# Two-layer graph attention, layer 0: the four small transfers of a tile are begun by GpSimd in its own queue, SyncE begins only the adjacency chunks

## Chip, cores and metric

The kernel runs on one core of one Trainium2 chip. The metric is the device time of one launch in microseconds (us).

## The reference

Two layers of graph attention over N = 8192 nodes of 128 features. The adjacency has about one edge in a thousand (eight per row).

```python
def _L0_gnn_ref(h, adj, Ws, Wt, Wc):
    Whs = h @ Ws
    Wht = h @ Wt
    e = jnp.einsum('nh,mh->nm', Whs, Wht)
    z = jnp.where(adj > 0, e, NEG)
    alpha = jax.nn.softmax(z, axis=-1)
    return alpha @ (h @ Wc)

def _L1_gnn_ref(h, adj, W, a):
    Wh = h @ W
    e = jax.nn.leaky_relu((Wh @ a[:128, 0])[:, None] + (Wh @ a[128:, 0])[None, :], negative_slope=0.2)
    attention = jax.nn.softmax(jnp.where(adj > 0, e, NEG_INF), axis=1)
    return jax.nn.elu(attention @ Wh)

h = jnp.maximum(_layernorm(x, axis=-1), 0.0)
x = x + _L0_gnn_ref(h, adj, L0_gnn_Ws, L0_gnn_Wt, L0_gnn_Wc)
h = jnp.maximum(_layernorm(x, axis=-1), 0.0)
x = x + _L1_gnn_ref(h, adj, L1_gnn_W, L1_gnn_a)
```

## The kernel before

**Stages.** The program first loads all rows of x, normalizes them and projects them (up to about 100 us). Then comes the stage that this change touches: layer 0 over 64 tiles of 128 query rows each (about 100 to 1088 us). After it the rows of layer 1 are prepared, and layer 1 runs over the same 64 tiles. Layer 1 doesn't read the adjacency again: layer 0 has stored, for every tile, which key blocks were picked (`sel_pick`) and the mask of the picked keys (`sel`).

**What a tile of layer 0 does.** A tile's adjacency, 128 queries by 8192 keys as int32, is 4 MB. It comes in four chunks of 1 MB (`load_chunk`, L394 to L398), into four buffers (`adj_st`). VectorE converts each chunk to 8 bits (`convert`, L1284). It reduces the tile to an indicator (L1290, one such instruction in a tile, so its start is a good mark for the tile's period), and makes a matrix `pick` from a prefix sum (L1307). TensorE uses `pick` to gather the keys (L650), values (L662) and mask (L677) that have an edge. ScalarE takes these from PSUM: keys L970, values L975, mask L982 (`take_mask`, two halves in a tile, into one of two buffers of `m_sel`). TensorE computes the scores (L694 to L699; their L696 reads the mask), VectorE reads them with their maximum (L1318), ScalarE takes the exponential (L990), TensorE turns the weights (L708, taken by L997) and weighs the values (L720), and VectorE writes the tile's result `y_t` (`finish`, L1361).

**Software pipeline.** Every engine runs `tile_sweep(engine, step)`: steps i = 0 to 66, where step i works on tile i in its front part, on tile i-1 in its middle part, on tile i-2 in its rear part and on tile i-3 in its ending. Steps 0 to 3 and 62 to 66 are written out, those between run in a hardware loop of two steps. The order within a step is written by hand and differs by engine. On VectorE it is: convert chunk 0 of tile i+1; indicate tile i; finish tile i-3; convert chunk 1; four tiny operations of tile i-2 and one that adds x (`without_edges`, L1352); place; read two scores of tile i-1; pick of tile i; convert chunks 2 and 3; read the other two scores.

**The four small transfers of a tile**, all begun by SyncE (SP) between the chunks:

- `store_y` (L406): `y_t` to `x_mid`, 64 KB, after `y_ready` (the finish of tile i-3);
- `load_x` (L401): x of tile i-1 to `x_t`, 64 KB, no wait;
- `store_pick` (L417): `pick` of tile i-1 to `sel_pick`, 256 KB, after `pick_ready`;
- `store_mask` (L411): `m_sel` of tile i-2 to `sel`, 256 KB, after `m_evac` (both halves of L982).

SP's order in a step:

```python
if later:
    load_chunk(i + 2, 0)
if ending(i):
    store_y(i - 3, 1 - b)
if later:
    load_chunk(i + 2, 1)
if within(i, 3, TILES + 1):
    load_x(i - 1, 1 - b)
if middle(i):
    store_pick(i - 1, 1 - b)
if rear(i):
    store_mask(i - 2, b)
if later:
    load_chunk(i + 2, 2)
    load_chunk(i + 2, 3)
```

A chunk load waits until VectorE has converted what was in its buffer. In the other direction ScalarE's `take_mask` waits for `m_out`: before it writes the first half of a tile's mask, the store of the mask two tiles before must have landed, since there are two buffers. Each of the other three has two buffers as well: `pick_out` is waited for by L1307, `y_out` by L1361, `x_in` by L1352. GpSimd (POOL) makes a few constants at the start (its last is L548) and then only waits for the end of the layer.

Of the kernel before, what the change touches and what calls it, by code (L numbers as in the profile page):

```python
# [16 lines left out]
P = 128  # L17
# [9 lines left out]
SLOPE = 0.2  # L27
EPS = 1e-5
# [12 lines left out]
def gnn_kernel(nc, x, adj, adjB, Ws, Wt, Wc, W1, a1, out, x_mid, sel, sel_pick):  # L41
    N = x.shape[0]
    TILES = N // P
# [10 lines left out]
    with ExitStack() as ctx:  # L54
# [253 lines left out]
        def within(t, lo, hi):  # L308

            return not isinstance(t, int) or lo <= t < hi  # L310
# [14 lines left out]
        def middle(i):  # L325
            return within(i, 1, TILES + 1)
# [4 lines left out]
        def ending(i):  # L331
            return within(i, 3, TILES + 3)
# [44 lines left out]
        def _(sp):  # L377
# [22 lines left out]
            def load_x(t, b):  # L400
                sp.dma_start(x_t[:, b, :], x[bass.ts(t, P), :]).then_inc(x_in[b], 16)  # L401

            def store_y(t, b):

                sp.wait_ge(y_ready, t + 1)
                sp.dma_start(x_mid[bass.ts(t, P), :], y_t[:, b, :]).then_inc(y_out[b], 16)  # L406

            def store_mask(t, b):

                sp.wait_ge(m_evac, t * 2 + 2)  # L410
                sp.dma_start(sel[bass.ds(t, 1), :, :].rearrange("o p n -> p (o n)"),  # L411
                             m_sel[:, b, :, :].rearrange("p s w -> p (s w)")).then_inc(m_out[b], 16)

            def store_pick(t, b):

                sp.wait_ge(pick_ready, t + 1)
                sp.dma_start(sel_pick[bass.ds(t, 1), :, :].rearrange("o p n -> p (o n)"), pick_w[:, b, :]  # L417
                             ).then_inc(pick_out[b], 16)

            def tile_io(i, b):  # L420
                later = within(i, 0, TILES - 2)
                if later:
                    load_chunk(i + 2, 0)
                if ending(i):
                    store_y(i - 3, 1 - b)
                if later:
                    load_chunk(i + 2, 1)
                if within(i, 3, TILES + 1):
                    load_x(i - 1, 1 - b)
                if middle(i):  # L430
                    store_pick(i - 1, 1 - b)
                if rear(i):
                    store_mask(i - 2, b)
                if later:
                    load_chunk(i + 2, 2)
                    load_chunk(i + 2, 3)
# [10 lines left out]
            load_x(0, 0)  # L447
            load_x(1, 1)
# [88 lines left out]
        def _(pool):  # L537
# [11 lines left out]

            def mask(tau, m):  # L550
# [17 lines left out]

            by_choice(pool, lambda: None, all_keys)
# [1117 lines left out]
```

## Time and profile before

| | us |
|---|---|
| three runs: median (lowest to highest) | 1651.59 (1649.45 to 1652.6) |
| the profiled execution, its own time | 1654.9 |
| its span, from first to last instruction | 1653.2 |
| busy: TensorE / VectorE / ScalarE / GpSimd | 1415.0 / 1447.7 / 893.3 / 1.5 |
| mean granted TensorE clock, as a share of full speed | 0.957 |
| bytes moved | 363.11 MB, mean 220 GB/s |

The profiled execution took 3.3 us more than the median, and 1.7 us more than its span. All transfers run on 16 DMA engines. All those that the program begins are in one queue, q1, which is SP's. Times in the sections that follow count from the span's start. "To landing" is the time from the start of the instruction that begins a transfer until its semaphore is complete.

### The profile page before, as it was taken

What the parts mean: (1) busy time and instruction counts of PE and PEld (TensorE: products, weight loads), DVE (VectorE), ACT (ScalarE), POOL (GpSimd) and SP (SyncE); (2) the same over time, 40 slices, a digit from 0 to 9 for tenths busy, and PEclk for the clock granted to TensorE, in tenths of its full rate; (3) what the DMA queues carried; (4) which work ended last, traced back from release to release, by engine and by line L of the source; (5) the groups of instructions that cost most, each with busy time, mean ns of one, the idle gap of its engine ahead of it and who ended that gap; (6) DMA issues with size and microseconds to landing.
All of it is one profiled execution on the core that took longest, in us unless ns stands there. A gap on an engine that the chain in (4) does not pass through costs nothing.

```text
span 1653.2 us, 78949 instructions
## 1 busy us (share of the span) xinstructions
PE 1415.0 (86%) x31882; PEld 1212.3 (73%) x32010; DVE 1447.7 (88%) x3171; ACT 893.3 (54%) x1872; POOL 1.5 (0%) x11
## 2 busy tenths in 40 slices
PE   2848899999999999899999999966888879889886
PEld 1536777777877788777877777744888878778776
DVE  5777799999999999999999999635999999999997
ACT  2725566666666666666666666666433333333332
POOL 0000000000000000000000000000000000000000
PEclk9968999999999999999999999979999989989988
DMA  6067799999999999999999999420332322332331
GB/s 211 0 259 252 281 326 320 326 330 324 319 340 329 327 328 314 331 325 330 328 326 332 330 327 322 139 57 6 106 95 84 98 91 81 92 92 80 97 91 44
DMA packets 114297, 363.11 MB, mean 220 GB/s; under 512 B 11504, under 2 KB 44528, under 8 KB 81392
## 3 DMA queue, kind: packets, MB, share of 16 engines
q1 hardware_dynamic: 114160, 361.02, 64.2%
q8 instruction: 118, 1.93, 0.5%
q14 instruction: 19, 0.16, 0.0%
HBM read 319.03 MB, written 41.94 MB: 218 GB/s over the span
## 4 chain that ended last, share of the span: by engine, by line
PE 34%; DVE 29%; issue 17%; DMA 12%; ACT 4%; DVEq 2%; SPq 2%; ACTq 0%
DMA sel<-arena 10%; PE ps L802 8%; DVE arena L1455 8%; PE ps L720 7%; DVE arena L1290 5%; DVE arena L1284 4%; PE ps L708 4%; PE ps L791 3%; DVE arena L1318 3%; PE ps L699 2%; PE ps L650 2%; DVE arena L1463 2%; PE ps L662 2%; PE ps L696 2%; ACT arena L990 2%
## 5 line engine op out<-in xcount | busy, mean ns | idle before, releaser
L1284 DVE TENSOR_SCALAR arena<-arena 128x2048 fp8e4<-128x2048 int32 x256 | 306.5, 1219 | 26.2 <-PE ps L677 14.0
L802 PE MATMUL ps<-arena 128*128 128x129 f32 x2048 | 266.1, 292 | 38.6 <-DVE arena L1463 38.5
L802 PEld LDWEIGHTS ps<-arena 128*128 128x128 f32 x2048 | 254.2, 205 | 48.8 <-DVE arena L1463 44.6
L1455 DVE TENSOR_SCALAR arena<-arena 128x128 f32 (+1 forms) x1024 | 268.4, 339 | 20.4 <-ACT arena L1039 20.4
L720 PE MATMUL ps<-arena 128*128 128x128 f32 x2048 | 271.6, 281 | 0.8 <-issue 0.8
L720 PEld LDWEIGHTS ps<-arena 128*128 128x128 f32 x2048 | 248.3, 192 | 4.3 <-issue 1.0
L970 ACT ACTIVATE arena<-ps 128x512 f16<-128x512 f32 x256 | 152.6, 596 | 180.0 <-PE ps L650 180.0
L997 ACT ACTIVATE arena<-ps 128x512 f32<-128x512 f32 x256 | 153.5, 600 | 130.3 <-PE ps L708 130.2
L1318 DVE CUSTOM_DVE_ANT_0 arena<-ps,arena 128x512 f32<-128x512 f32 x256 | 168.6, 686 | 19.5 <-PE ps L699 16.5
L791 PE MATMUL ps<-arena 128*32 128x131 f16 x8192 | 156.6, 228 | 32.6 <-issue 21.6
L1039 ACT ACTIVATE arena<-ps 128x393 f32<-128x393 f32 (+1 forms) x384 | 149.2, 462 | 49.6 <-PE ps L791 49.3
L791 PEld LDWEIGHTS ps<-arena 128*32 128x32 fp8e4 x8192 | 133.2, 99 | 52.3 <-issue 37.1
L662 PE MATMUL ps<-arena 128*32 128x128 f16 x8192 | 164.4, 222 | 6.3 <-issue 6.3
L708 PE MATMUL ps<-ident,arena 128*128 128x128 f32 x1024 | 162.9, 282 | 7.0 <-ACT arena L990 2.6
L650 PEld LDWEIGHTS ps<-arena 128*128 128x128 f16 x4096 | 130.8, 96 | 51.4 <-issue 9.0
L1047 ACT ACTIVATE arena<-ps 128x129 f32<-128x129 f32 x64 | 17.9, 279 | 271.1 <-PE ps L802 266.2
L699 PE MATMUL ps<-arena 128*128 128x512 f16 x512 | 155.8, 387 | 3.9 <-issue 3.9
L975 ACT ACTIVATE arena<-ps 128x512 f32<-128x512 f32 x256 | 152.3, 595 | 0.4 <-PE ps L662 0.4
L1463 DVE SCALAR_TENSOR_TENSOR arena<-arena 128x1024 f32<-128x1024 fp8e4 x128 | 150.5, 1216 | 0.0
L650 PE MATMUL ps<-arena 128*128 128x32 fp8e4 x4096 | 144.6, 177 | 6.7 <-DVE arena L1307 3.8
L990 ACT ACTIVATE arena<-arena,neg_max 128x1024 f32<-128x1024 f32 x128 | 146.0, 1141 | 4.4 <-DVE neg_max L1328 4.4
L1307 DVE TENSOR_TENSOR arena<-arena 128x2048 fp8e4<-128x2048 f16 x64 | 146.3, 2286 | 0.1
(139 smaller groups left out, 1537.4 us busy)
## 6 DMA issues: line engine op xcount, KB each, us to landing
arena<-in_adjB SPq DMA_DIRECT2D x256, 1024.0 KB, 7.6
sel_pick<-arena SPq DMA_DIRECT2D x64, 256.0 KB, 8.0
sel<-arena SPq DMA_DIRECT2D x64, 256.0 KB, 8.0
arena<-sel_pick SPq DMA_DIRECT2D x64, 256.0 KB, 3.1
arena<-sel SPq DMA_DIRECT2D x64, 256.0 KB, 2.7
x_t<-in_x SPq DMA_DIRECT2D x64, 64.0 KB, 7.9
x_mid<-y_t SPq DMA_DIRECT2D x64, 64.0 KB, 4.8
arena<-x_mid SPq DMA_DIRECT2D x8, 512.0 KB, 4.4
```

Of the source, the lines that this page charges most:

```text
L650: last = nc.tensor.matmul(kg_ps[:, k * SLOT:(k + 1) * SLOT], kp[:, g * SB + k, :], pick[:, b, g * SB + k, :], start=True, stop=True)
L662: last = nc.tensor.matmul(vg_ps[g % 2][j * SLOT:(j + 1) * SLOT, s * D:(s + 1) * D], pick[:, b, k, :], c_vals[:, k, l * D:(l + 1) * D], sta ...
L699: last = nc.tensor.matmul(dst, rows[:, bass.ts(t, P)], k_sel[:, q * GW:(q + 1) * GW], start=False, stop=(n == 1), skip_group_check=True)
L708: last = nc.tensor.transpose(pt_ps[:, k * P:(k + 1) * P], zc[:, (4 * g + k) * P:(4 * g + k + 1) * P], ident[:, :])
L720: last = nc.tensor.matmul(pv_ps, p_T[:, g % 2, k * P:(k + 1) * P], v_sel[:, b, s, :], start=(s == 0), stop=(s == SB - 1), skip_group_check ...
L791: last = nc.tensor.matmul(xg_ps[g % 3][j * SLOT:(j + 1) * SLOT, at:at + XW], pick[:, b, s * QB + j, :], wv[:, s * QB + j, l, :], start=(l ...
L802: last = nc.tensor.matmul(xv_ps[b], w_msk[:, b, s, :], x1_sel[:, b, s, 0:VW], start=(s == 0), stop=(s == SB - 1))
L990: nc.scalar.activation(half, half, ACT.Exp, bias=neg_max[:, 0:1], scale=1.0 / SCORE, accum_out=sums[:, 0, h:h + 1]).then_inc(p_done, 1)
L1284: nc.vector.tensor_scalar(mask_8[:, b, c * QCH:(c + 1) * QCH, :], adj_st[:, c, :, :], 0.0, 1.0, ALU.is_gt, ALU.add, saturate=False).then_i ...
L1318: nc.vector.tensor_tensor_reduce(out=zc[:, q * GW:(q + 1) * GW], in0=s_ps[q % 2], in1=zero_b, scale=1.0, scalar=LOWEST, op0=ALU.subtract, ...
L1455: last = nc.vector.tensor_scalar(w_raw[:, s, :], own, x1_sel[:, b, s, D + 2:D + 3], x1_sel[:, b, s, D + 1:D + 2], ALU.mult, ALU.max)
L1463: nc.vector.scalar_tensor_tensor(w_msk[:, b, at, :], m_in8[:, b, at, :], -1.0, w_raw[:, at, :], ALU.add, ALU.mult).then_inc(w_ready, 1)
```

## The change

SP's step keeps the four chunks alone. The four helpers move to GpSimd's program, in the same order among themselves, with the same waits, and GpSimd runs them in the same `tile_sweep`. Ahead of each transfer stands an increment of a semaphore that nobody in this stage waits for (`pool_settled`). The first two loads of x are begun by GpSimd after its constants, where SP began them behind the chunks of tile 0. Two constants (`SHIFT`, `TINY`) are added and not used.

```diff
             def tile_io(i, b):
-                later = within(i, 0, TILES - 2)
-                if later:
-                    load_chunk(i + 2, 0)
-                if ending(i):
-                    store_y(i - 3, 1 - b)
-                if later:
-                    load_chunk(i + 2, 1)
-                if within(i, 3, TILES + 1):
-                    load_x(i - 1, 1 - b)
-                if middle(i):
-                    store_pick(i - 1, 1 - b)
-                if rear(i):
-                    store_mask(i - 2, b)
-                if later:
-                    load_chunk(i + 2, 2)
-                    load_chunk(i + 2, 3)
+                if within(i, 0, TILES - 2):
+                    for c in range(4):
+                        load_chunk(i + 2, c)
...
             for c in range(4):
                 load_chunk(0, c)
-            load_x(0, 0)
-            load_x(1, 1)
             sp.wait_ge(mean_ready, 1)
...
             nc.gpsimd.memset(bounds[:, :], 0.0).then_inc(const_pool, 1)
 
+            def load_x(t, b):
+                pool.sem_inc(pool_settled, 1)
+                pool.dma_start(x_t[:, b, :], x[bass.ts(t, P), :]).then_inc(x_in[b], 16)
+
+            def store_y(t, b):
+
+                pool.wait_ge(y_ready, t + 1)
+                pool.sem_inc(pool_settled, 1)
+                pool.dma_start(x_mid[bass.ts(t, P), :], y_t[:, b, :]).then_inc(y_out[b], 16)
+
+            def store_mask(t, b):
+
+                pool.wait_ge(m_evac, t * 2 + 2)
+                pool.sem_inc(pool_settled, 1)
+                pool.dma_start(sel[bass.ds(t, 1), :, :].rearrange("o p n -> p (o n)"),
+                             m_sel[:, b, :, :].rearrange("p s w -> p (s w)")).then_inc(m_out[b], 16)
+
+            def store_pick(t, b):
+
+                pool.wait_ge(pick_ready, t + 1)
+                pool.sem_inc(pool_settled, 1)
+                pool.dma_start(sel_pick[bass.ds(t, 1), :, :].rearrange("o p n -> p (o n)"), pick_w[:, b, :]
+                             ).then_inc(pick_out[b], 16)
+
+            def tile_io(i, b):
+                if ending(i):
+                    store_y(i - 3, 1 - b)
+                if within(i, 3, TILES + 1):
+                    load_x(i - 1, 1 - b)
+                if middle(i):
+                    store_pick(i - 1, 1 - b)
+                if rear(i):
+                    store_mask(i - 2, b)
...
+            load_x(0, 0)
+            load_x(1, 1)
+            tile_sweep(pool, tile_io)
             by_choice(pool, lambda: None, all_keys)
```

How it moves instructions. SP before, one step of the hardware loop from the y store to the mask's store (`in_adjB` are the chunks, `arena` the large buffer in SBUF that holds most tiles; an ISA or REGISTER_ALU row is a wait or the working out of an address). Ahead of these rows stands chunk 0, behind them chunks 2 and 3:

```order
L406 ISA [waits y_ready]
L406 DMA x_mid<-y_t 128x128
L306 REGISTER_ALU
L398 ISA [waits conv_done]
L398 DMA arena<-in_adjB 128x2048
L401 ISA
L401 DMA x_t<-in_x 128x128
L417 ISA [waits pick_ready]
L417 DMA sel_pick<-arena 128x1024
L410 ISA
L411 ISA [waits m_evac]
L411 DMA sel<-arena 128x1024
```

The change, SP, the first two chunks of the same step (line numbers are those of the changed kernel). The other two read alike:

```order
L400 ISA [waits conv_done]
L400 DMA arena<-in_adjB 128x2048
L308 REGISTER_ALU
L400 ISA [waits conv_done]
L400 DMA arena<-in_adjB 128x2048
```

SP keeps only loads that wait for VectorE's conversions; nothing on it waits for `y_ready`, `pick_ready` or `m_evac` any more. The change, POOL, the same step (before, POOL had nothing in this stage):

```order
L525 ISA [waits y_ready]
L525 DMA x_mid<-y_t 128x128
L519 ISA
L519 DMA x_t<-in_x 128x128
L538 ISA [waits pick_ready]
L538 DMA sel_pick<-arena 128x1024
L529 ISA
L531 ISA [waits m_evac]
L531 DMA sel<-arena 128x1024
```

The four transfers stand in one row on POOL, and the mask's is the last of them; all four stand behind the wait for `y_ready`.

## Rows read from the trace of the kernel before

**Rows 1.** Page part 2: rates over the span in 40 slices of 41.3 us.

```profile
PE   2848899999999999899999999966888879889886
DVE  5777799999999999999999999635999999999997
POOL 0000000000000000000000000000000000000000
DMA  6067799999999999999999999420332322332331
GB/s 211 0 259 252 281 326 320 326 330 324 319 340 329 327 328 314 331 325 330 328 326 332 330 327 322 139 57 6 106 95 84 98 91 81 92 92 80 97 91 44
```

**Rows 2.** Windows: length, busy by engine (PE, PEld, DVE, ACT, POOL), clock, DMA share, GB/s.

```profile
102.45:203.25 100.80, 76.67 (x1771) 62.86 (x1783) 77.09 (x131) 48.17 (x88) 0.00 (x0) 0.83 0.80 295
203.25:1034.13 830.88, 779.22 (x18536) 654.38 (x18644) 772.54 (x1458) 543.03 (x1008) 0.00 (x0) 1.00 0.94 327
```

**Rows 3.** Source L1290, 203 to 1035 us: min/median/max ns, first and last start.

```profile
L1290 DVE TENSOR_REDUCE arena<-arena x57: 2276/2278/2280, 203.2 to 1034.1; 128x64 f32<-128x2048 f32 x57
```

**Rows 4.** Waits, 203.25 to 1034.13 us: us in total, times, longest.

```profile
ACT arena L982 <- DMA sel<-arena: 53.8, 47, 2.2
PE ps L696 <- ACT arena L982: 39.7, 38, 1.9
...
DVE arena L1284 <- PE ps L677: 12.8, 28, 0.7
```

**Rows 5.** Timeline of VectorE, four tiles: start us, us, what.

```profile
589.03 2.28 DVE L1290 TENSOR_REDUCE arena<-arena 128x64 f32<-128x2048 f32 x1
...
603.52 2.28 DVE L1290 TENSOR_REDUCE arena<-arena 128x64 f32<-128x2048 f32 x1
...
618.23 2.28 DVE L1290 TENSOR_REDUCE arena<-arena 128x64 f32<-128x2048 f32 x1
...
620.93 0.35 DVE L1361 SCALAR_TENSOR_TENSOR y_t<-ps,inv,u_t 128x128 f32<-128x128 f32 x1 [0.19 <-issue]
...
621.64 1.21 DVE L1284 TENSOR_SCALAR arena<-arena 128x2048 fp8e4<-128x2048 int32 x1
...
627.45 2.36 DVE L1284 TENSOR_SCALAR arena<-arena 128x2048 fp8e4<-128x2048 int32 x2
...
632.73 2.28 DVE L1290 TENSOR_REDUCE arena<-arena 128x64 f32<-128x2048 f32 x1
```

**Rows 6.** Timeline of SP, one step.

```profile
621.47 0.36 SPq L406 DMA_DIRECT2D x_mid<-y_t  x1
623.01 0.33 SPq L398 DMA_DIRECT2D arena<-in_adjB  x1
623.56 0.33 SPq L401 DMA_DIRECT2D x_t<-in_x  x1
624.08 0.36 SPq L417 DMA_DIRECT2D sel_pick<-arena  x1
624.73 0.43 SPq L411 DMA_DIRECT2D sel<-arena  x1
```

**Rows 7.** Chain of waits in order of time: start us, us, what.

```profile
624.73 8.62 DMA sel<-arena
...
648.52 2.29 DVE arena L1290
...
651.22 0.36 DVE y_t L1361
```

**Rows 8.** Timeline of ScalarE: idle before it and its releaser in brackets.

```profile
633.38 0.60 ACT L982 ACTIVATE arena<-ps 128x512 f16<-128x512 f32 x1 [2.14 <-DMA sel<-arena]
```

**Rows 9.** Tile sel, 203 to 1034 us: issue ns min/median/max, then landing times.

```profile
L411 SPq DMA_DIRECT2D sel<-arena x56: 355/356/1390, 209.8 to 1025.0; - x56
...
DMA to landing us min/median/max: 5.6/8.1/8.8
```

**Rows 10.** Page part 6, transfers: count, KB each, median us to landing.

```profile
arena<-in_adjB SPq DMA_DIRECT2D x256, 1024.0 KB, 7.6
...
arena<-sel SPq DMA_DIRECT2D x64, 256.0 KB, 2.7
x_t<-in_x SPq DMA_DIRECT2D x64, 64.0 KB, 7.9
x_mid<-y_t SPq DMA_DIRECT2D x64, 64.0 KB, 4.8
```

**Rows 11.** Lines, 203.25 to 1034.13 us: busy us, mean ns | idle before.

```profile
L1284 DVE TENSOR_SCALAR arena<-arena 128x2048 fp8e4<-128x2048 int32 x225 | 269.4, 1218 | 21.8 <-PE ps L677 12.8 <-issue 9.0
```

**Rows 12.** Chain of waits at the stage's end.

```profile
1086.50 0.36 DVE y_t L1361
1086.88 1.53 DMA x_mid<-y_t
1088.54 6.26 DMA arena<-x_mid
```

More of the change, by code:

```diff
@@ L27 @@
 SLOPE = 0.2
+SHIFT = 50.0
+TINY = 1e-30
 EPS = 1e-5
@@ L398, in load_chunk @@
                 sp.dma_start(adj_st[:, c, :, :], rows).then_inc(adj_in[c], 16)
[L400 to L418, printed above, removed]
-            def tile_io(i, b):
-                later = within(i, 0, TILES - 2)
-                if later:
-                    load_chunk(i + 2, 0)
-                if ending(i):
-                    store_y(i - 3, 1 - b)
-                if later:
-                    load_chunk(i + 2, 1)
-                if within(i, 3, TILES + 1):
-                    load_x(i - 1, 1 - b)
-                if middle(i):
-                    store_pick(i - 1, 1 - b)
-                if rear(i):
-                    store_mask(i - 2, b)
-                if later:
-                    load_chunk(i + 2, 2)
-                    load_chunk(i + 2, 3)
+            def tile_io(i, b):
+                if within(i, 0, TILES - 2):
+                    for c in range(4):
+                        load_chunk(i + 2, c)
                 if isinstance(i, int) and i == TILES:
```

## The prediction

> **What bounds the kernel now.** I read the slices first, to see which stage the change can reach. From slice 6 to 25 VectorE and TensorE are both nine tenths busy or more, the DMA engines too, and some 326 GB/s are moved; GpSimd is idle [rows 1]. This is layer 0. Layer 1 behind it moves a third of that, and none of its transfers are changed. So the question is the period of a tile in layer 0.
>
> The windows and the one L1290 of each tile give it. From 203.25 to 1034.13 us there are 57 of them, so 56 periods in 830.88 us: **14.84 us a tile** [rows 2, 3]. VectorE is busy 772.54 us of these (93%), TensorE 779.22 (94%). Which of them is waited for, and on what, is told by the waits: the only thing besides TensorE, VectorE and ScalarE that an engine waits for in these 56 tiles is the store of the mask. ScalarE's L982 stands 53.8 us in 47 tiles until the store of two tiles before has landed, and TensorE's scores stand behind it for 39.7 us [rows 4]. VectorE doesn't wait for a chunk once.
>
> A few tiles in a row show what such a wait is worth. They begin at 589.03, 603.52, 618.23, 632.73 and 648.52 us [rows 5, 7]: periods of 14.49, 14.71, 14.50 and 15.79. In the last, L982 had stood 2.14 us [rows 8]. Nineteen of the 56 periods read 14.49 or 14.50 and none is shorter, so **14.49 is what the engines take when the mask doesn't hold them**.
>
> Now the loop that passes through the store. The finish L1361 of one step ends at 621.28 [rows 5]. SP, which waits for it before it goes on, begins the mask's store at 624.73, behind the y store, chunk 1, x and the pick [rows 6]. It lands 8.62 us later [rows 7], L982 starts at 633.38 [rows 8], and the finish two steps further ends at 651.58 [rows 7]. With L for the time from the finish to the landing (here 12.1 us), two periods are at least L + 18.2 us, the 18.2 being 651.58 less 633.38. It costs nothing while L is under 2 x 14.49 - 18.2 = **10.8 us**; beyond that each us of L costs half a us a tile. The formula holds on the mean: 3.45 us to the issue plus the median landing of 8.1 [rows 9] is L = 11.55 and a period of 14.88, against 14.84 measured.
>
> **The change, part by part.**
>
> *SP loses four transfers of about 0.36 us each and their waits.* Worth nothing by itself: chunk 1 went out 0.16 us after its conversion had ended (622.85 to 623.01), the other chunks wait for conversions as well [rows 5, 6], and VectorE never waits for a chunk. A chunk takes 7.6 us of the 13 or so that it has, so it may also become some us slower for nothing.
>
> *GpSimd gains four transfers a tile, one behind the other.* No row shows GpSimd beginning one. Below, it costs what SP's do, 0.36 us; above, the slowest issue of this store on SP, 1.39 us [rows 9]. I take 0.9, the middle, since no row is nearer to the one end than to the other. Four are 3.6 us of 14.84 on an idle engine. GpSimd wakes about 0.2 us after the finish, as SP does [rows 5, 6].
>
> *GpSimd and VectorE.* VectorE converts chunk 1 from 0.36 us after the finish on, for 1.21 us, and chunks 2 and 3 from 6.2 to 8.5 us after it [rows 5]. The conversion passes 2048 values in 1218 ns, where L1290 takes 2278 for as many [rows 3, 11]: it runs at twice the pace of the others. The trace of before can't show what GpSimd's beginning of transfers does beside such an instruction; below it is nothing, above each waits for the other's end. I take 1.2 us of delay for GpSimd (the length of one conversion) and none for VectorE. The Trainium skill (SBUF — State Buffer, the section on SBUF's two separate sides) says that such a VectorE instruction locks GpSimd out of a shared port, so that a transfer begun by GpSimd gets no descriptors until it ends. That speaks against this change. By this rule alone the sum stays as it is, because four conversions never cover more than 2.4 us in one piece; that VectorE is held as well is the first rival.
>
> *The mask's landing.* Before, it stands in one queue behind chunks of 1 MB: it and x both land after 8 us, although x is a quarter of its size, and only the y store, begun with less ahead of it, takes 4.8 [rows 9, 10]. It is queueing. In a queue of its own it has the pick's 256 KB ahead of it and not the chunks. Below: 2.7 us, the time of as large a load in layer 1, where the engines are free. Above: 8.8, the slowest of before. I take 5.6, the fastest that this store ever had in the stage, since the 16 engines still carry the same bytes. The Trainium skill (DMA: Bandwidth & Descriptors, the section on issuing engines not being separate DMA queues) says that beginning transfers from several engines saves only the time to begin them, all of them running interleaved on the same 16 engines. By it the landing stays at 8.1, which is priced as the second rival.
>
> *The sum.* L = 0.2 + 1.2 + 3 x 0.9 + 5.6 = **9.7 us**, 1.1 under the 10.8 from which it costs. The period is then 14.49, and 830.88 - 56 x 14.49 = **19.4 us** less. At the low ends L is 0.2 + 3 x 0.36 + 2.7 = 4.0, with the same gain, since 14.49 is a floor: the gain can't be larger by this route. At the high ends, with chunks 2 and 3 in the way too, L = 0.2 + 1.2 + 2.4 + 3 x 1.39 + 8.8 = 16.8, the period 17.5, and the stage 149 us longer.
>
> *Next bound.* At 14.49 the stage needs 327 x 14.84 / 14.49 = 335 GB/s; one slice moved 340 [rows 1]. It would just do.
>
> *The other waits that moved.* The pick, y and x of a tile have a whole period until they are asked for, 14 us against at most 9: nothing. The first steps (102 to 203 us) run under start-up waits of TensorE, DMA share 0.80 [rows 2]: nothing. At the end the last y store and the reload of its rows are on the chain, 1.53 us from the finish to landing [rows 12]; with GpSimd's 0.9 instead of SP's 0.33 this is 0.6 us more. Together **-18.8 us**: 1654.9 becomes 1636.1 for an execution like the profiled one, and against the median, which lies 3.3 lower, 1651.6 - 18.8 = 1632.8, say 1633.
>
> **The rivals.**
>
> 1. *VectorE is held by GpSimd* (slower). If beginning a transfer keeps a conversion from starting, the y store, begun 0.2 us after the finish, holds chunk 1's conversion, due at 0.36, until 1.1: 0.74 us a tile. The floor of 14.49 becomes 15.23, 0.39 over today's, 56 x 0.39 = +22 us: 1674. It decides from 0.35 us a tile. For it: the timing, which is tight in every tile, and a VectorE that is 93% busy. Against: nothing in the trace, GpSimd does nothing there.
> 2. *The mask lands no sooner* (slower). A queue of its own doesn't help, because the 16 engines that serve it are busy with the chunks all the same, and GpSimd begins the mask as its fourth transfer. With a landing of 8.1 as before, L = 0.2 + 1.2 + 2.7 + 8.1 = 12.2, period 15.2, 56 x 0.36 = +20 us: 1672. With transfers that also take 1.39 us each to begin, L = 13.7, period 15.95, +62 us: 1714. It decides from L = 11.5, that is at a landing of 7.4 with my other terms. For it: the DMA share of 0.94 [rows 2]. Against: the y store's 4.8 us, begun with less in its queue on the same busy engines [rows 10].
> 3. *No change*: the terms cancel, L is near 11.5 and the period near 14.84, or the engines can't give more than 327 GB/s: 1652. For it: the same share of 0.94. Against: the slice with 340 GB/s.
>
> **How the numbers follow.** Forecast 0.50, rival 1 0.20, rival 2 0.20, rival 3 0.10. A measurement of this kernel can tell 0.2%, 3.3 us, from no change. Rival 3 is a little wider than that, by 0.01 on either side, which gives faster 0.51, same 0.08, slower 0.41. The likeliest case by itself spans 1626 to 1642 (some us from the start-up steps, which I priced at nothing, below; L up to 11.1 above). The range goes from 1625 up to 1690: that takes in rivals 1 and 3 and the milder half of rival 2 (L up to 12.8), and leaves out some 0.17.
>
> **What would show it.** Right: the wait of L982 for `sel<-arena` falls from 53.8 us to a few, the L1290 stand 14.5 apart, `sel` lands after 4 to 6 us, and L1284 stays at 1218 ns. Rival 1: L1284 longer than 1218 ns or idle before it, and periods over 15 without a wait for the mask. Rival 2: L982 waits over 2 us in every tile, POOL's transfers stand over a us apart. Wrong altogether: chunks that VectorE waits for, at a DMA share near 1. The terms with the least behind them are the 0.9 us and the 5.6 us.

## The result: 0.6% slower, and the profile after

The changed kernel takes 1662.3 us (median of 11 runs, 1651.05 to 1671.32), the kernel before, run beside it, 1651.59 (11 runs, 1644.01 to 1664.42). The ratio is **1.0059, 95% interval 1.0032 to 1.0086**: slower by about 10 us, where I had forecast 19 us less. The profiled execution took 1658.5 us, its span 1657.0.

The page of the changed kernel, parts 2 and 3: GpSimd is now a tenth busy through the stage, it has a queue of its own, q0, with 42 MB, and the rate in the stage is hardly changed from [rows 1] and [rows 2]: 323 GB/s from 203.25 to 1034.13 us, where it was 327.

```profile
POOL 0000111111111111111111111100000000000000
DMA  6068899999989999998899999410322332332321
GB/s 211 0 261 304 277 334 322 326 326 333 324 304 323 334 321 324 324 325 314 299 320 333 332 327 319 160 36 0 107 86 89 98 98 78 93 92 80 96 88 48
...
q1 hardware_dynamic: 77296, 319.06, 56.9%
q0 software_dynamic: 14336, 41.96, 6.7%
```

Its waits from 203.25 to 1034.13 us, the same window as [rows 4] (the lines have moved by four: L986 was L982, L698 and L700 were L694 and L696). The wait that should have gone is there, in fewer and longer pieces: 52.3 us in 39 waits, the longest 4.8, against 53.8 in 47 and at most 2.2.

```profile
ACT arena L986 <- DMA sel<-arena: 52.3, 39, 4.8
PEld ps L698 <- ACT arena L986: 39.0, 32, 4.5
PE ps L698 <- ACT arena L986: 33.5, 31, 4.3
```

The mask's store by itself (tile sel, the same window, against [rows 9]), and the four transfers in the page's part 6 (against [rows 10]): the mask still lands after more than 8 us, with a maximum of 11.7 instead of 8.8. To begin a transfer takes GpSimd 0.54 us.

```profile
L531 POOL DMA_DIRECT2D sel<-arena x55: 539/539/542, 217.1 to 1026.8; - x55
...
DMA to landing us min/median/max: 5.4/8.3/11.7
```

```profile
sel_pick<-arena POOLq DMA_DIRECT2D x64, 256.0 KB, 8.2
sel<-arena POOLq DMA_DIRECT2D x64, 256.0 KB, 8.2
...
x_t<-in_x POOLq DMA_DIRECT2D x64, 64.0 KB, 6.6
x_mid<-y_t POOLq DMA_DIRECT2D x64, 64.0 KB, 5.2
```

One step in the timelines of VectorE and GpSimd, to be read against [rows 5, 6]: the finish ends at 601.13, the four transfers begin at 601.88, 602.81, 603.44 and 604.13. So the mask's store begins 3.00 us after the finish; that is also the median, where SP took 3.45.

```profile
600.78 0.35 DVE L1365 SCALAR_TENSOR_TENSOR y_t<-ps,inv,u_t 128x128 f32<-128x128 f32 x1
...
601.49 1.21 DVE L1288 TENSOR_SCALAR arena<-arena 128x2048 fp8e4<-128x2048 int32 x1
```

```profile
601.88 0.94 POOL L525 DMA_DIRECT2D x_mid<-y_t  x1 [11.63 <-DVE y_t L1365]
602.81 0.54 POOL L519 DMA_DIRECT2D x_t<-in_x  x1
603.44 0.54 POOL L538 DMA_DIRECT2D sel_pick<-arena  x1
604.13 0.54 POOL L531 DMA_DIRECT2D sel<-arena  x1
```

**Where the stage loses time.** In each trace I took the starts of the one big reduction of a tile (L1290 before, L1294 after), from the seventh tile to the one nearest 1020 us. Their mean distance is 14.83 us before and 14.99 after: 56 x 0.16 = 9 us. The whole stage from the seventh tile to the 63rd takes 830.9 us before and 841.1 after. The 10 us of the result are the difference of two medians. The two profiled executions are only 3.8 us apart in span, because the seventh tile begins 6.6 us earlier after the change (196.6 for 203.3); the start-up is taken up under the prediction below. Most distances are alike in both, 14.5 to 15.9. What is new are tiles like these three (windows of the changed kernel between two such starts; columns as in [rows 2]):

```profile
448.08:465.47 17.39, 15.83 (x336) 12.96 (x337) 13.91 (x27) 11.14 (x21) 2.55 (x4) 0.90 0.90 312
465.47:479.97 14.50, 13.88 (x333) 11.70 (x330) 13.77 (x27) 8.18 (x17) 2.53 (x4) 1.00 0.85 295
...
809.92:830.12 20.20, 16.29 (x336) 13.11 (x337) 13.92 (x28) 11.15 (x21) 2.55 (x4) 0.83 0.81 282
```

The tile of 17.39 us had stood 2.46 us for its mask, the one of 20.20 us 4.82. TensorE's clock is 0.90 and 0.83 of full in them, and 1.00 in the tile between. The chain of waits shows the long one: the store begun at 801.41 landed after 11.74 us. TensorE's timeline in the first of the two tiles shows what the clock does. After 1.95 us without work (this is the part of the wait that TensorE saw) the same two matmuls of L703 take 1.06 us at first and 0.60 when next run, 2.6 us later: part of the time it ran at 1.2 GHz instead of 2.4. The granted clock of the tile says the same (0.90 over 17.39 us).

```profile
801.41 11.74 DMA sel<-arena
```

```profile
449.64 0.61 PE L698 MATMUL ps<-arena 128*128 128x512 bf16 x1 [1.95 <-ACT arena L986]
450.04 0.63 PE L700 MATMUL ps<-arena 128*128 128x128 bf16 x4
450.47 1.06 PE L703 MATMUL ps<-arena 128*128 128x512 f16 x2
...
453.03 0.60 PE L703 MATMUL ps<-arena 128*128 128x512 f16 x2
```

Compared with a tile whose wait was a little shorter and whose clock stayed full (2.02 us, period 15.86, so 0.66 us less over 14.50 than it had waited), the tile of 2.46 should have taken 16.3 and took 17.4: about 1.1 us are the clock's. In e5, the changed kernel's second trace, two tiles with waits of 2.30 and 2.25 us took 15.87 us at a clock of 1.00 and 17.19 at 0.90, so 1.3 us there. The four tiles over 16 us in this window hold 13.9 us over the 14.57 that tiles take with no such wait (below). All 55 hold 23.

### The profile page after: what moved, and what is told of

It is laid out like the page before. It is cut to its first block, busy times and chain, and to the rows that moved or that the text cites. A ratio compares the mean times of both kernels' runs of the same rounds, so it can differ in the third digit from the quotient of the medians.

```text
span 1657.0 us, 79396 instructions
## 1 busy us (share of the span) xinstructions
PE 1429.5 (86%) x32010; PEld 1213.4 (73%) x32010; DVE 1447.1 (87%) x3171; ACT 891.6 (54%) x1872; POOL 163.3 (10%) x267
## 4 chain that ended last, share of the span: by engine, by line
PE 39%; DVE 27%; issue 17%; DMA 11%; ACT 4%; DVEq 2%; POOL 1%; ACTq 0%; POOLq 0%; SPq 0%
DMA sel<-arena 9%; PE ps L806 9%; PE ps L724 8%; DVE arena L1459 7%; DVE arena L1294 5%; PE ps L712 4%; PE ps L795 3%; PE ps L703 3%; DVE arena L1322 3%; PE ps L666 3%; PE ps L654 2%; DVE arena L1288 2%; DVE arena L1467 2%; PE ps L698 2%; PE ps L700 1%
## 5 line engine op out<-in xcount | busy, mean ns | idle before, releaser
L1288 DVE TENSOR_SCALAR arena<-arena 128x2048 fp8e4<-128x2048 int32 x256 | 306.6, 1220 | 26.4 <-PE ps L681 13.4
L806 PE MATMUL ps<-arena 128*128 128x129 f32 x2048 | 261.9, 289 | 38.9 <-DVE arena L1467 38.8
L1459 DVE TENSOR_SCALAR arena<-arena 128x128 f32 (+1 forms) x1024 | 268.7, 343 | 18.2 <-ACT arena L1043 18.1
L703 PE MATMUL ps<-arena 128*128 128x512 f16 x512 | 156.5, 388 | 2.3 <-issue 2.3
```

The source lines that it names most:

```text
L703: last = nc.tensor.matmul(dst, rows[:, bass.ts(t, P)], k_sel[:, q * GW:(q + 1) * GW], start=False, stop=(n == 1), skip_group_check=True)
L806: last = nc.tensor.matmul(xv_ps[b], w_msk[:, b, s, :], x1_sel[:, b, s, 0:VW], start=(s == 0), stop=(s == SB - 1))
L1288: nc.vector.tensor_scalar(mask_8[:, b, c * QCH:(c + 1) * QCH, :], adj_st[:, c, :, :], 0.0, 1.0, ALU.is_gt, ALU.add, saturate=False).then_i ...
L1459: last = nc.vector.tensor_scalar(w_raw[:, s, :], own, x1_sel[:, b, s, D + 2:D + 3], x1_sel[:, b, s, D + 1:D + 2], ALU.mult, ALU.max)
```

## Experiments

Fifteen runs follow, in four jobs, two of them of the unedited kernels; ratios are to the kernel before, run in the same job. For reading them, L is the time from the finish to the mask's landing. The floor of a tile, which I had put at 14.49 us, is 14.57 (see e2).

### e1: the mask first, in GpSimd's queue

```diff
             def tile_io(i, b):
+                if rear(i):
+                    store_mask(i - 2, b)
                 if ending(i):
                     store_y(i - 3, 1 - b)
...
-                if rear(i):
-                    store_mask(i - 2, b)
```

> The changed kernel with GpSimd's order in a step turned: the mask's store first (it waits only for its own data, ready since the step before), then y, x, pick. Theory A (all of the loss in the 64 tiles is the wait of ScalarE's L986 for the mask's landing, and the clock that drops behind the long waits): that wait goes to about 0, the tiles stand 14.5 us apart instead of 14.99, the clock stays at 1.00, and the time is 56 x 0.49 = 27 us under the changed kernel's 1662, near 1635, ratio to the kernel before 0.99. Theory B (transfers begun by GpSimd cost by themselves, through slower DMA engines or a slower VectorE): the wait goes as well, but periods stay above 14.7 and the time above 1645, with VectorE waiting for chunks.

Measured: 1637.42 us, ratio **0.988 (0.984 to 0.992)**, mean period 14.56. No row of the waits has an engine waiting for the mask's landing (the first is GpSimd waiting for ScalarE to make the mask); those of ScalarE are the ones for TensorE that every tile has. Theory A holds. By theory B the period would have stayed over 14.7.

```profile
POOL sel L531 <- ACT arena L986: 204.8, 55, 3.8
ACT arena L1001 <- PE ps L712: 141.9, 167, 1.8
ACT arena L974 <- PE ps L654: 134.7, 56, 2.4
PEld ps L690 <- issue: 29.3, 55, 0.6
```

### e2: the mask first, on SP

```diff
                 later = within(i, 0, TILES - 2)
+                if rear(i):
+                    store_mask(i - 2, b)
                 if later:
                     load_chunk(i + 2, 0)
...
-                if rear(i):
-                    store_mask(i - 2, b)
```

> The kernel before with SP's order in a step turned: the mask's store ahead of chunk 0 instead of behind the pick, everything still on SP. Theory A: the wait of L982 (53.8 us) goes to about 0, periods 14.5, 19 us less than before, about 1632. Against the first kernel of this job it tells what the queue alone costs once the mask holds nobody: by theory A the two are within 0.3% of each other, by theory B this one is faster by 10 us or more.

Measured: 1639.59 us, ratio **0.989 (0.985 to 0.993)**, mean period 14.56, the wait gone. With the mask out of the way the queue makes no difference that can be measured: GpSimd's transfers cost nothing by themselves that shows, and SP's cost nothing either. The same gain was to be had by moving two lines, with no change of queue. The periods here alternate between 14.50 and 14.64, one of each per turn of the two-step loop, so the floor is 14.57 and not the 14.49 that I had read from the shortest.

### e3: the mask alone in GpSimd's queue

```diff
-                if rear(i):
-                    store_mask(i - 2, b)
...
+            def tile_io(i, b):
+                if ending(i):
+                    pool.wait_ge(y_ready, i - 2)
+                if rear(i):
+                    store_mask(i - 2, b)
```

> The kernel before with only the mask's store on GpSimd; GpSimd still waits for the finish of tile i-3 first, so that the store begins at about the time of before. Theory C (in its own queue the mask waits for what GpSimd has put ahead of it, the 256 KB of the pick, at the small share that chunk packets of 8 KB leave): with nothing ahead it lands after about 5 us instead of 8.3, begins some 0.3 us after the finish, L is near 5.5, the wait is 0, the period 14.5 and the time near 1635. Theory D (the landing is set by the 16 engines' backlog or by the software queue's own latency, whatever is ahead): it lands after 7.5 us or more.

Measured: 1635.04 us, ratio 0.986 (0.981 to 0.991). The store begins 0.81 us after the finish and lands after a median of 5.9 (3.6 to 8.2): L = 6.7, no wait, period 14.56. With nothing ahead in its queue it is 2.4 us faster than in the changed kernel. This is near the 5.6 that I had assumed for the change, where 64, 64 and 256 KB stand ahead. But this store is also begun 2.2 us earlier in the step than the changed kernel's (0.81 for 3.00), and when it is begun matters too (e6, e7 and e11).

### e4 and e10: chunks cut in halves, in either arrangement

```diff
-                rows = adjB[bass.ds(t, 1), :, c * QCH:(c + 1) * QCH, :].rearrange("o p b n -> p (o b) n")
-                sp.dma_start(adj_st[:, c, :, :], rows).then_inc(adj_in[c], 16)
+                for k in range(2):
+                    lo = c * QCH + k * (QCH // 2)
+                    rows = adjB[bass.ds(t, 1), :, lo:lo + QCH // 2, :].rearrange("o p b n -> p (o b) n")
+                    sp.dma_start(adj_st[:, c, k * (QCH // 2):(k + 1) * (QCH // 2), :], rows).then_inc(adj_in[c], 16)
```

> The changed kernel, each 1 MB chunk loaded as two transfers of 512 KB, so that a partition's piece is 4 KB instead of 8. Theory C (DMA engines alternate between the two queues packet by packet): GpSimd's packets wait for half as much at each turn, the mask's landing falls from 8.3 to about 6, the wait of L986 from 52 us to under 15, periods to 14.6, the time to about 1645. Theory D (backlog or latency): landing within 0.5 us of 8.3 and the time within 5 us of 1662. If smaller packets cost the engines throughput, the DMA share rises and VectorE waits for chunks, and the time is over 1665.

Measured on the changed kernel: 1637.82 us, ratio 0.987 (0.981 to 0.993), landing 6.9 us, wait 13.6 us, period 14.57. That looked like theory C. But the control, the same cut on the kernel before:

> The kernel before with each chunk loaded as two transfers of 512 KB; all on SP. It is the control for e4, where the same cut made the mask in GpSimd's queue land after 6.9 us instead of 8.3. Theory C (engines alternate between queues packet by packet, so smaller chunk packets help only what stands in another queue): in one queue the cut changes nothing, the mask lands after 8.0 us, ratio 0.997 to 1.006. Rival (pieces of 4 KB are simply moved faster, or the halves let the load end earlier): landing near 7, L982's wait under 20 us, ratio 0.99.

Measured: 1638.27 us, ratio **0.991 (0.988 to 0.994)**, landing 6.1 us instead of 8.0, wait 20.7 us, period 14.57. The rival of that expectation holds: the landing falls by 1.9 us with a single queue, where e4's fell by 1.5 (8.4 to 6.9). So e4 says nothing for sharing by packets. That pieces of 4 KB a partition bring the mask home earlier is shown in both; why, is not. The row of e10, with the DMA share at 0.95 and all bytes the same:

```profile
DMA to landing us min/median/max: 4.4/6.1/7.4
```

### e5: the changed kernel again

> The changed kernel once more, unedited, so that its 64 tiles are seen in a second trace beside the other kernels of this job. All theories: about 1662, ratio 1.003 to 1.01. Theory E (the loss is in a few long waits): again most periods read 14.5 to 14.7, a handful read over 16.5, each of these behind a mask that landed after more than 9 us, and TensorE's granted clock falls below 1.00 there. Theory F (an even slowing): no period far above the mean.

Measured: 1658.47 us, ratio 1.0054 (1.0021 to 1.0088), mean period 14.94. Five periods read over 16 (16.41 to 17.70), and the sum of the waits is only 43.8 us. Theory E, with two parts of the expectation not met. The mask of these tiles doesn't always land after more than 9 us; the longest landing here is 9.8. And the clock didn't fall in all five: the tile of 16.41 us had TensorE idle for 2.55 us, longer than in any of the other four, at a clock of 1.00.

```profile
388.36:405.55 17.19, 15.41 (x333) 12.91 (x337) 13.91 (x27) 11.15 (x21) 2.56 (x4) 0.90 0.90 313
420.05:435.92 15.87, 13.97 (x333) 11.82 (x337) 13.92 (x28) 11.03 (x20) 2.56 (x4) 1.00 0.95 341
836.73:853.14 16.41, 13.97 (x333) 11.81 (x337) 13.91 (x27) 11.14 (x21) 2.56 (x4) 1.00 0.93 320
```

### e6: y, mask, x, pick

```diff
                 if ending(i):
                     store_y(i - 3, 1 - b)
+                if rear(i):
+                    store_mask(i - 2, b)
...
-                if rear(i):
-                    store_mask(i - 2, b)
```

> The changed kernel with GpSimd's order y, mask, x, pick instead of y, x, pick, mask. The mask's store still waits for the finish, but has only the y store ahead of it: it begins about 1.2 us earlier, 1.5 to 1.8 us after the finish. Theory C (the mask waits for the pick ahead of it in its own queue, at the share that chunk packets leave): it lands after 5.5 to 6.5 us, L is about 8, no wait that costs, periods 14.57, time near 1637. Theory D (backlog or latency of the software queue): it still lands after 8.3; L is then about 10, which is just under the threshold, so the time also falls; the landing time decides between them, not the total.

Measured: 1640.15 us, ratio **0.991 (0.988 to 0.994)**, so about 1.5% less than the changed kernel by exchanging transfers within one queue. The store begins 1.68 us after the finish, 1.3 earlier, and lands after 7.2: L = 8.9. The landing lies between the two theories' numbers (5.5 to 6.5 and 8.3), so it decides for neither.

### e7: pick and mask on GpSimd

```diff
+                if ending(i):
+                    pool.wait_ge(y_ready, i - 2)
+                if middle(i):
+                    store_pick(i - 1, 1 - b)
+                if rear(i):
+                    store_mask(i - 2, b)
```

> Pick's and mask's stores on GpSimd, pick first, both behind the wait for the finish; y and x stay on SP. Beside e3, in which the mask had nothing ahead and landed after 5.9 us, it adds only the pick. Theory C: the mask lands after 7.5 to 8.5 us; it begins some 1.7 us after the finish, L is near 9.7, under 10.8, so periods are 14.6 and the time 1635 to 1645. Theory D: 5.9 us as in e3.

Measured: 1632.97 us, ratio 0.990 (0.984 to 0.996). The pick lands after 5.9 us, as the mask alone did in e3, and the mask, now behind it, after 7.5. Begun at 1.68, L = 9.2; the wait is 1.7 us in all. Theory C's number holds (7.5 to 8.5), and the landing is 1.6 us longer than in e3. But the store is also begun 0.9 us later than there. In e6 it begins at the same 1.68 us with 64 KB ahead instead of 256, and lands only 0.3 us sooner, after 7.2. So these runs don't separate what stands ahead in the queue from the moment at which the store is begun.

### e8: mask on SP, the others on GpSimd

```diff
                 for c in range(4):
                     if within(i, 0, TILES - 2):
                         load_chunk(i + 2, c)
+                    if c == 1 and rear(i):
+                        store_mask(i - 2, b)
```

> The changed kernel with the mask's store back on SP, behind chunk 1 (so it begins about 2 us after the finish); y, x and pick stay on GpSimd. It stands behind chunks again, while the pick goes past in the other queue. Theory C: it lands after 7 to 8.5 us, as the chunks ahead of it lose a part of the engines to the pick; L is 9 to 10.5, under the threshold, periods 14.6 and time near 1640. If the mask is slower on SP than in GpSimd's queue by more than a us, L passes 10.8 and the time is over 1650.

Measured: 1652.45 us, ratio 0.999 (0.996 to 1.002). It begins 2.37 us after the finish and lands after **9.0**, a us later than in the kernel before, in spite of three transfers fewer in its own queue. So a queue of its own for the other three doesn't clear the way for it. That their packets take turns from it is the likely reason; it is not shown apart from its earlier beginning (2.37 for 3.45). L = 11.4, wait 49.6 us, mean period 14.94. Theory C's landing (7 to 8.5) and time (1640) are missed. L and the time came out as in the last sentence of the expectation, though not its condition: the mask was 0.7 us slower than in GpSimd's queue (8.3), not over 1.

### e9: the mask one place later

```diff
                 if later:
                     load_chunk(i + 2, 2)
+                if rear(i):
+                    store_mask(i - 2, b)
+                if later:
                     load_chunk(i + 2, 3)
```

> The kernel before with the mask's store one place later on SP, behind chunk 2, whose own wait lets it go only about 7.6 us after the finish instead of 3.45. Theory A in numbers (two periods are at least L + 18.2 us, L from the finish to the mask's landing; and behind the longest waits TensorE runs part of the tile at half its clock, 1.3 us more): with a landing of 6 to 8 us L is 13.6 to 15.6, periods 15.9 to 16.9 from the loop alone, 0.7 more where the clock falls in every second tile, so 60 to 150 us over the kernel before, clock near 0.90 in the tiles with the wait. Rival (the wait for the mask is only where the time is booked, and the 16 engines' rate is what sets the period): under 20 us slower, DMA share still 0.94.

Measured: 1739.9 us (two runs), ratio **1.054 (1.047 to 1.061)**. The store begins 9.19 us after the finish and lands after 5.2, L = 14.4. The loop gives (14.4 + 18.2) / 2 = 16.3 us a tile, the trace 16.46, so the clock's part is smaller than the 0.7 expected. The window 205 to 1020 us and the wait:

```profile
205.00:1020.00 815.00, 730.00 (x16494) 596.82 (x16496) 691.32 (x1291) 482.17 (x893) 0.00 (x0) 0.96 0.81 294
```

```profile
ACT arena L983 <- DMA sel<-arena: 107.6, 49, 3.1
```

The DMA engines have dropped to 0.81 and 294 GB/s: they don't set the period, they follow it. And in the less crowded queue the landing is short. This loop damps itself, which is one reason why large delays of the mask cost less than they seem to.

### e11 and e13: the mask alone on ScalarE's queue, whole and in two

```diff
                     take_turned(c, 0)
                     exps(c, 1)
+                    store_mask(c, b)
```

> The kernel before with only the mask's store taken off SP and begun by ScalarE, behind the second exponential of the tile, which is about 0.9 us after the finish, as in e3. Theory C (what helps is a queue with nothing ahead, whoever owns it): it lands after 5 to 6.5 us as in e3 (5.9), the wait goes to 0, ratio 0.985 to 0.992; ScalarE's 0.36 us for it is hidden in its idle time. Rival G (GpSimd's software queue is served in some better way than SP's kind of queue): it lands after 7.5 us or more, and still the wait would be small, as L is under 9.

Measured: 1633.28 us, ratio 0.988 (0.985 to 0.992). The landing is 7.5 us, so with nothing of its own ahead it is no sooner than e7's. My placing was off: in the trace the store begins 1.6 us before the finish instead of 0.9 after it, at another moment of the chunk traffic than e3, and so the two landings can't be set against each other. L is 5.9, and no wait is left. The cut into two transfers of 1 KB a partition:

> e11 (mask alone, begun by ScalarE, 9 packets a transfer on each engine, landed after 7.5 us) with the mask cut into two transfers of 128 KB, 1 KB from each partition: as many bytes, twice as many packets. Theory P (an engine takes one packet from each queue in turn, so a transfer needs as many turns as it has packets, each as long as a chunk packet of 8 KB, 0.4 us): the second half lands 10 to 11 us after the first was begun. Theory D (bytes or backlog): both halves are there after 7.5 to 8.5 us.

Measured: 1630.65 us (two runs), ratio 0.985 (0.979 to 0.991). The packets in ScalarE's queue doubled for the same bytes:

```profile
q10 hardware_dynamic: 8064, 14.68, 4.7%
```

```profile
q10 hardware_dynamic: 16130, 14.69, 5.2%
```

The first is e11, the second e13. All 112 landings of e13 lie under 7.9 us (median 6.4), and the second half is begun 0.49 us behind the first: both are there after at most 8.4 us, where theory P wanted 10 to 11. The number of packets doesn't lengthen the landing here; theory D's number holds.

### e14: the same cut in GpSimd's queue

> e3 (mask alone, begun by GpSimd, 5 packets a transfer on each engine, landed after 5.9 us) with the same cut. If GpSimd's queue packs rows up to 4 KB, the number of packets that carry data stays 4. Theory P: the second half lands after 5 to 6.5 us by its own count, about 7 after the first was begun; the difference to e13 is over 2.5 us. Theory D: both kernels lengthen alike.

Measured: 1633.65 us (two runs), ratio 0.987 (0.981 to 0.992), median landing 6.0 us, maximum 7.8; e3 had 5.9 and 8.2. No longer either, so it doesn't tell the theories apart; e13 does.

### e12: SP's start-up order

```diff
+                if isinstance(i, int) and i < 4:
+                    for c in range(4):
+                        load_chunk(i + 2, c)
+                    later = False
```

> The kernel before with SP's order changed in the four steps written out at the start alone: there it begins the four chunks of a step before the small transfers. In all traces with the four small ones on GpSimd the seventh tile begins at 195.3 to 200.1 us, in the two with everything on SP at 202.4 and 203.3. Theory S (at the start, SP stands in waits for the finish, the pick and the mask while chunk loads wait behind them): the seventh tile begins near 197.5, chunks of steps 0 to 3 go out as soon as converted, and the time is 5 us under the kernel before, ratio 0.997. Rival (noise of the start, or the code's loading): the seventh tile at 202 or later, ratio 0.999 to 1.001.

Measured: 1657.46 us, ratio 1.004 (1.001 to 1.007), the seventh tile at 206.25 us. Theory S is wrong, and the time is a little above the rival's range as well. Behind its start-up this kernel is the one before, so that it gives one more look at the 64 tiles: mean period 14.84, two over 16 us, one of them (17.31) with a clock of 0.90.

### e15: the kernel before again

> The kernel before, unedited, for a second trace of its 64 tiles. Theory E (the changed kernel loses by few long waits and the clock behind them, the sum of the waits being about the same): here again the sum is near 54 us, at most two periods in 56 read over 16 us, and the mean period is 14.80 to 14.86, against 14.99 and 14.94 in the two traces of the changed kernel.

Measured: 1651.15 us, ratio 0.999 (0.996 to 1.002), mean period 14.80, wait 45.5 us. Two periods over 16 us, and these two have the clock of 0.90 too:

```profile
391.74:408.97 17.23, 15.80 (x336) 12.94 (x337) 13.91 (x28) 11.16 (x21) 0.00 (x0) 0.90 0.92 324
541.78:558.89 17.11, 15.84 (x336) 12.93 (x337) 13.92 (x27) 11.13 (x21) 0.00 (x0) 0.90 0.90 320
```

So the fall of the clock is in the kernel before as well. Over the whole stage, the clock fell in 0, 2 and 1 tiles in its two traces and e12's, and in 5 and 4 in the changed kernel's, 3 in e8. Single waits for the mask of over 2 us number 4, 5 and 5 against 7 and 7, with 7 in e8. So a wait of that length doesn't always bring the clock down, and in e9 it did so in 19 tiles of 37.

### All in one table

From the traces, 205 to 1020 us: median us from the finish to the mask's beginning, median landing, their sum L, the wait for the mask in 815 us; the mean period as above; and the ratio.

| kernel | begins | lands | L | wait | period | ratio |
|---|---|---|---|---|---|---|
| e3 alone, GpSimd | 0.81 | 5.9 | 6.7 | 0 | 14.56 | 0.986 |
| e6 second of four | 1.68 | 7.2 | 8.9 | 0.5 | 14.56 | 0.991 |
| e7 behind pick | 1.68 | 7.5 | 9.2 | 1.7 | 14.56 | 0.990 |
| e4 changed, half chunks | 3.00 | 6.9 | 9.9 | 13.6 | 14.57 | 0.987 |
| e10 before, half chunks | 3.92 | 6.1 | 10.0 | 20.7 | 14.57 | 0.991 |
| changed (e5) | 3.00 | 8.4 (8.0) | 11.4 (11.0) | 50.1 (43.8) | 14.99 (14.94) | 1.006 (1.005) |
| before (e15) | 3.45 | 8.0 (7.8) | 11.5 (11.3) | 53.3 (45.5) | 14.83 (14.80) | 1 |
| e8 mask on SP | 2.37 | 9.0 | 11.4 | 49.6 | 14.94 | 0.999 |
| e9 late | 9.19 | 5.2 | 14.4 | 107.6 | 16.46 | 1.054 |

Up to L = 10 nothing is lost, from about 11 on it is. e1, e2, e11 and e13 have the mask home well before it is asked for and stand at 14.56.

## Why the prediction was wrong

**The bound and the loop: right.** That ScalarE's wait for the mask was all that the stage had to give, and that the stage's period follows from L to within 0.2 us a tile, came out in every kernel. e9 is the dose in the other direction. The gain forecast for a mask in time (19 us) was measured as 20 in e1 and 17 in e2 by their medians; in the stage of the traces it is some 15. The floor was 14.57 and not 14.49: I took the shorter of two alternating periods for both, which is 4.5 us too much in 56 tiles. (Twenty of the 56 periods read 14.49 or 14.50, not nineteen; nothing hangs on it.)

**GpSimd's four transfers: right in size.** I summed 0.2 + 1.2 + 3 x 0.9 = 4.1 us to the mask's beginning; it was 3.0. A transfer takes 0.54 us to begin, not 0.9, and the conversion held the first for 0.4 us, not 1.2. Only the wake-up was longer, 0.75 us for 0.2.

**The step that failed: "I take 5.6, the fastest that this store ever had in the stage."** The landing was 8.3 us. This one term kept L at 11.4 instead of 9.7, over the 10.8 from which it costs (the beginning, 3.0 for 4.1, took 1.1 of the error back). I had the right row before me: x lands as late as the mask, which is queueing; but I took the queue for SP's own. I took the fastest landing that the store ever had, without a row for a second queue on busy engines, and sent 384 KB ahead of the mask in it. The landing came near the assumed number only in e3, alone in GpSimd's queue and begun early (5.9). With y alone ahead it was 7.2 (e6), with the pick ahead 7.5 (e7), alone in ScalarE's queue 7.5 (e11), and back on SP, with the others moved away, 9.0 (e8). So a new queue by itself doesn't free a transfer from the load on the engines. How much of the 8.3 us is the 384 KB ahead, and how much the moment at which the store is begun, stays open. With 8.3 in my sum L is 12.4, and my own formula gives 15.3. It says slower; rival 2 had been priced with nearly this number, 8.1, and at 0.20 I had it too low.

**Rival 2** is the one whose reason happened: the mask lands no sooner. Its price didn't. The mask is begun 1.1 us earlier than I had priced it, L is 11.4 and not 12.2, and at 11.4 the formula gives 14.8 us a tile, which is rival 3's "no change". That the time rose by 10 us all the same doesn't follow from the mean L of any rival (see the clock, below); its direction agreeing with rival 2's is partly luck. Rival 2's reasoning held: the 16 engines are busy whichever queue asks. The Trainium skill's rule that transfers begun from several engines run interleaved on the same 16, and that this saves only the time to begin them (DMA: Bandwidth & Descriptors, on issuing engines), describes this case better than my number did: 3.45 became 3.00 us, 8.1 became 8.3. e3's landing of 5.9 us is less than the rule by itself would lead one to expect.

**What the formula lacked: the clock.** By L alone (11.4 and 11.0 after, 11.5 and 11.3 before) the changed kernel should have been level or a little ahead. It is behind because more of its waits are long: 7 and 7 of over 2 us, against 4 and 5. In the first trace the mask lands after 5.4 to 11.7 us, where it was 5.6 to 8.8. Behind some of the long waits TensorE runs at half its clock for a part of the tile. Five tiles in each of its traces read over 16 us (one of the first trace's lies behind 1020 us), against none and two before. At 1.1 to 1.3 us for a fall (two of them in the tile of 20.20 us, by its clock of 0.83), an estimate from the tiles above, the clock explains about 7 of the 10.2 us that the stage lost from the first trace of before to the first of after, and 2 to 3 of the 6.8 from e15 to e5. The rest is the long waits themselves. That these tiles make the difference is read from two traces of either kernel, not forced in an experiment.

**Rival 1** (VectorE held) didn't happen. L1288 takes 1219 ns where it took 1218 [rows 11], with 21.0 us idle before it against 21.8:

```profile
L1288 DVE TENSOR_SCALAR arena<-arena 128x2048 fp8e4<-128x2048 int32 x222 | 265.9, 1219 | 21.0 <-PE ps L681 11.1 <-issue 9.9
```

Its condition wasn't met, either. I had GpSimd begin at 0.2 us and the conversion at 0.36; in fact GpSimd comes at 0.75, so the conversion is always first. What a transfer begun just ahead of a conversion does to it, no run here shows.

**Start-up, priced at nothing:** the seventh tile begins at 195.3 to 200.1 us in the nine traces with a transfer on GpSimd, and at 197.4 to 206.3 in the eight without. That may be some 4 us in the change's favour; e12 tried one cause and missed. It is open. The stage's loss less this gain is 3.6 us from before to after (10.2 less 6.6) and 2.4 us from e15 to e5 (6.8 less 4.4), where the medians lie 10 and 6 us apart. Where the rest of that comes from, the traces don't show.

## What to carry to other kernels

A store that frees one of two buffers has a deadline. Before moving it to another queue, look in the order written out for what it waits behind without need: here the mask was ready some 12 us before it was stored, and putting it first in the same queue (e2) gave 1.1%, where the new queue cost 0.6%. Price a transfer in a new queue by the engines' load and by what is sent ahead of it there, not by the queue being new; and when a wait sits near the point from which it costs, ask for its spread, because a fall of TensorE's clock can make the long ones dearer than their length.

## What the runs showed of the hardware that I had not expected

- **A conversion holds GpSimd's transfer to the end and 0.12 us beyond.** Begun 0.39 us into VectorE's conversion of 601.49 to 602.70, the y store was through at 602.82. The Trainium skill (SBUF — State Buffer, on SBUF's two sides) has this rule, with about 115 ns after VectorE's end, and the trace agrees. The 0.12 us is the same for every y store of the stage, here and in e5. It cost 0.4 us of GpSimd's time a tile (0.94 instead of 0.54), and none of it mattered.
- **Halves of a chunk, 4 KB a partition instead of 8, bring the small transfers home sooner** in a queue that is 0.94 to 0.95 busy: the mask after 6.1 instead of 8.0 us, x after 5.9 instead of 7.9, with the same bytes. It was worth 0.9% to the kernel before. Unexplained.
- **Twice the packets for the same bytes cost no time** in a second queue (e11, e13).
- **TensorE's clock can fall after less than 2 us without work**, to a mean of 0.90 over the tile, in a stage where it is otherwise 1.00. Each of the 15 falls in the traces of before, after, e5, e8, e12 and e15 comes in, or within 1.5 us of, a stretch of 1.6 to 4.3 us in which TensorE stood idle. Not each such stretch brings one: in e5 one of 2.55 us left the clock at 1.00.
- The best kernels (e3, e7, e11, e13, e14, and with them e1, e2 and e4) lie at ratios of 0.985 to 0.990, and their intervals overlap. All stand on the floor of 14.56 us a tile, so which of them is the fastest can't be told here, and there is nothing more to be had from these transfers.
